# Score tiles as four matmuls of 32 columns, and the maximum pass's causal mask in 64-row matmuls

## What is computed

```python
def ffn(h):                       # weights are +1/-1 from booleans, widths 256 -> 1024 -> 1024 -> 256
    h = relu(s0 * (concat(h, -h) @ sign(k0))) * 2
    h = relu(s1 * (h @ sign(k1))) * 2
    return s2 * (h @ sign(k2))
def attn(h):                      # q, k, v: 16 heads of 16
    scores = where(causal, -1e9, q @ k.T / sqrt(16))
    return (softmax(scores) @ v) @ w_o.T + b_o
x = x + 0.5 * ffn(layernorm(x))
x = x + attn(layernorm(x))
x = x + 0.5 * ffn(layernorm(x))
```

## Time and profile before

| | |
|---|---|
| timed runs | 1733.23, 1733.54, 1737.15 us |
| profiled execution, first to last instruction | span 1730.6 us |
| TensorE matmul busy | 1669.8 us, 96% |
| VectorE busy | 1161.4 us, 67% |
| ScalarE busy | 959.1 us, 55% |
| GpSimd busy | 159.8 us, 9% |
| mean granted TensorE clock | 0.987 |
| attention stretch | 475 to 1348.8 us of the span |

### The profile page before, as it was taken

One profiled execution on the slowest core, in us unless ns is written; L12 is line 12 of the kernel. 1 busy time (PEld: TensorE's weight loads), 2 busy tenths in 40 slices (PEclk: granted clock), 3 DMA queues, 4 the chain that ended last, 5 costly groups with the idle time before them and its releaser, 6 DMA issues.

```text
span 1730.6 us, 31369 instructions
## 1 busy us (share of the span) xinstructions
PE 1669.8 (96%) x9872; PEld 691.9 (40%) x9872; DVE 1161.4 (67%) x1746; ACT 959.1 (55%) x1703; POOL 159.8 (9%) x310
## 2 busy tenths in 40 slices
PE   6899999999999999999999999999999799999999
PEld 3455555554522222222222222222223355555554
DVE  7535554455588887887887878878887566666632
ACT  2223322232288887888887878878888322222221
POOL 5100000000011110111111111011111000000000
PEclk9999999999999999999999999999999899999999
DMA  5011013110222201221122202221123111112000
GB/s 167 0 49 49 24 24 85 48 48 0 84 70 56 56 29 49 62 56 35 42 56 57 62 19 52 62 57 46 33 53 110 69 49 49 48 48 101 20 6 19
DMA packets 115754, 88.83 MB, mean 51 GB/s; under 512 B 76080, under 2 KB 95152, under 8 KB 115632
## 3 DMA queue, kind: packets, MB, share of 16 engines
q1 hardware_dynamic: 115632, 87.20, 17.3%
HBM read 49.15 MB, written 37.75 MB: 50 GB/s over the span
## 4 chain that ended last, share of the span: by engine, by line
PE 93%; DVE 3%; DMA 1%; issue 1%; SPq 1%; ACT 0%; DVEq 0%
PE ffn_mm L399 25%; PE ffn_mm L1184 17%; PE ffn_mm L1203 16%; PE ffn_mm L387 7%; PE ffn_acc L415 6%; PE ffn_acc L567 5%; PE ffn_tr L567 5%; PE ffn_mm L664 3%; PE ffn_tr L571 2%; PE ffn_acc L676 2%; PE ffn_acc L487 1%; PE ffn_tr L374 1%; PE ffn_acc L571 1%; DVE qk L1263 1%; DVE m_part L586 1%
## 5 line engine op out<-in xcount | busy, mean ns | idle before, releaser
L1145 ACT ACTIVATE probs<-ffn_mm,exp_scale 128x512 f32<-128x512 f32 (+3 forms) x1280 | 715.3, 636 | 134.8 <-PE ffn_mm L1184 129.0
L586 DVE TENSOR_REDUCE m_part<-ffn_acc 128x2 f32<-128x1024 f32 (+1 forms) x314 | 351.1, 1118 | 96.9 <-PE ffn_acc L567 53.4
L1184 PE MATMUL ffn_mm<-qk 66*128 66x512 f16 (+7 forms) x1280 | 389.5, 358 | 17.8 <-issue 14.1
L399 PE MATMUL ffn_mm<-ffn_h1h,w 128*128 128x512 f16 x1024 | 389.4, 380 | 7.7 <-DVE ffn_h2l L452 7.7
L399 PE MATMUL ffn_mm<-ffn_h1l,w 128*128 128x512 f16 x1024 | 389.3, 380 | 0.0
L586 DVE TENSOR_REDUCE m_part<-ffn_tr 128x2 f32<-128x1024 f32 (+3 forms) x326 | 328.0, 1006 | 40.7 <-PE ffn_tr L571 27.0
L1203 PE MATMUL ffn_mm<-probs,v 128*32 128x512 f32 (+3 forms) x2560 | 315.6, 550 | 0.3
L445 ACT ACTIVATE ffn_h2h<-ffn_mm 128x512 f16<-128x512 f32 x128 | 76.1, 597 | 309.5 <-PE ffn_mm L399 294.7
L1184 PEld LDWEIGHTS ffn_mm<-qk 66*128 66x128 f16 (+1 forms) x1280 | 103.8, 97 | 303.7 <-ACT probs L1145 232.1
L452 DVE SCALAR_TENSOR_TENSOR ffn_h2l<-ffn_mm,ffn_h2h 128x512 f16<-128x512 f32 x128 | 86.2, 686 | 191.6 <-ACT ffn_h2h L445 191.6
L1098 POOL TENSOR_SCALAR_AFFINE_SELECT probs<-probs 128x256 f32<-128x256 f32 (+1 forms) x256 | 109.8, 429 | 782.5 <-ACT probs L1145 782.4
(11 more groups left out here) (95 smaller groups left out, 1080.4 us busy)
## 6 DMA issues: line engine op xcount, KB each, us to landing
qk<-qk_scr SPq DMA_DIRECT2D x256, 64.0 KB, 2.7
ctx_scr<-ctx_out SPq DMA_DIRECT2D x64, 256.0 KB, 2.4
qk<-ctx_scr SPq DMA_DIRECT2D x64, 256.0 KB
v_scr<-v_pad SPq DMA_DIRECT2D x32, 256.0 KB, 2.9
v<-v_scr SPq DMA_DIRECT2D x16, 512.0 KB, 4.5
x_res<-L_attn_x SPq DMA_DIRECT2D x8, 512.0 KB, 3.6
qk_scr<-qk_hi SPq DMA_DIRECT2D x32, 128.0 KB, 1.8
qk_scr<-qk_lo SPq DMA_DIRECT2D x32, 128.0 KB, 1.8
```

What stands on the lines that cost most here:

```text
L399: ins = nc.tensor.matmul(f.mm[:, m % 4, :], w1[:, kt, m * P:(m + 1) * P], part[:, kt, :], start=(kt == 0 and part is f.h1h), stop=(kt == H ...
L586: nc.vector.tensor_reduce(m_part[u][:, t, :, r], s_ps[slot][:, :, 0:w], AX.X, ALU.max).then_inc(sb.s_done, 1)
L1145: nc.scalar.activation(probs[:, g % P_SLOTS, j, c0:CH], st_ps[bank(k)][:, c0:CH], ACT.Exp, scale=exp_scale[:, 0:1]).then_inc(se.exp_done, 1)
L1184: nc.tensor.matmul(st_ps[bank(k)][:, c0:CH], k_part(u, h, rows, slice(kb * P, (kb + 1) * P)), q_part(u, h, rows, slice(i * CH + c0, (i + 1 ...
```

## The change

Three edits. The score matmul of the second pass becomes four matmuls, each with 32 of the 128 keys as output columns, at column positions 0, 32, 64, 96, with the same moving operand and into the same bank; the semaphore is counted up on the last. The mask matmuls of the maximum pass become 64-row matmuls in each head's own rows, two halves for each head, with operands `pick_row` and `mask_row` in place of `ident_mask` and `mask`: four matmuls where there were two. GpSimd builds those operands after its other constants, and TensorE waits for them before the last feed-forward chunk; `mask` lives only in the first stage.

```diff
--- before.py
+++ after.py
@@ -120,6 +120,7 @@
 
         self.zero = new("zero")
         self.consts = new("consts")
+        self.pick = new("pick")
         self.vones = new("vones")
 
         self.sgn = new("sgn")
@@ -273,8 +274,8 @@
         bo_row = sbuf(top, "bo_row", [P, D], F32)
         ident = sbuf(top, "ident", [P, P], F32)
         ident_h = sbuf(top, "ident_h", [P, P], F16)
-        ident_mask = sbuf(top, "ident_mask", [P, P], F16)
-        mask = sbuf(top, "mask", [P, P], F16)
+        pick_row = sbuf(top, "pick_row", [P, 2, P], F16)
+        mask_row = sbuf(top, "mask_row", [P, 2, P], F16)
         ffn_scale = sbuf(top, "ffn_scale", [P, 1], F32)
         qk_scale = sbuf(top, "qk_scale", [P, 2], F32)
         exp_scale = sbuf(top, "exp_scale", [P, 1], F32)
@@ -567,9 +568,10 @@
                     ins = nc.tensor.matmul(s_ps[slot][:, h, 0:w], q_part(u, h, HEAD_ROWS[h], slice(t * P, (t + 1) * P)),
                                            k_part(u, h, HEAD_ROWS[h], slice(r * CH, r * CH + w)), start=True, stop=(r < i))
                 if r == i:
-                    for h in range(2):
-                        ins = nc.tensor.matmul(s_ps[slot][:, h, w - P:w], ident_mask[:, :], mask[:, :],
-                                               start=False, stop=True)
+                    for hf in range(2):
+                        for h in range(2):
+                            ins = nc.tensor.matmul(s_ps[slot][:, h, w - P:w], pick_row[HEAD_ROWS[h], hf, :],
+                                                   mask_row[HEAD_ROWS[h], hf, :], start=False, stop=(hf == 1))
             else:
                 wait(nc.tensor, sb.m_cols, cols)
                 ins = nc.tensor.matmul(s_ps[slot][0:4 * TPC, 0, 0:P], m_col.rearrange("p h a t -> p (h a t)"), ident_h[:, :],
@@ -621,6 +623,7 @@
             w_in = sbuf(st, "w_in", [P, 4, DT, D], F32)
             w_diff = sbuf(st, "w_diff", [P, DT, HID], F16)
             s_in = sbuf(st, "s_in", [P, 3], F32)
+            mask = sbuf(st, "mask", [P, P], F16)
             sgn = sbuf(st, "sgn", [P, 3], F32)
             s_abs = sbuf(st, "s_abs", [P, 3], F32)
             s_prod = sbuf(st, "s_prod", [P, 2], F32)
@@ -763,7 +766,6 @@
                                         pattern=[[-1, P]], channel_multiplier=1).then_inc(se.consts, 1)
                 pool.wait_ge(se.consts, 2)
                 nc.gpsimd.tensor_copy(ident_h[:, :], ident[:, :]).then_inc(se.consts, 1)
-                nc.gpsimd.tensor_scalar(ident_mask[:, :], ident[:, :], MASK_A, 0.0, ALU.mult, ALU.add).then_inc(se.consts, 1)
 
                 pool.wait_ge(se.k1_in, 16)
                 pool.wait_ge(se.sprep, 3)
@@ -782,6 +784,19 @@
                 pool.wait_ge(sb.rows_zero, 4)
                 for u in range(2):
                     nc.gpsimd.memset(k_part(u, 1, SHIFT_ROWS[1], slice(0, SEQ)), M_SCALE).then_inc(sb.rows_const, 1)
+
+                lo, hi = HEAD_ROWS
+                nc.gpsimd.memset(pick_row[:, :, :], 0.0).then_inc(se.pick, 1)
+                nc.gpsimd.memset(mask_row[:, :, :], 0.0).then_inc(se.pick, 1)
+                pool.wait_ge(se.pick, 2)
+                nc.gpsimd.memset(mask_row[hi, 0, 64:P], MASK_B).then_inc(se.pick, 1)
+                pool.wait_ge(se.pick, 3)
+                for n, (rows, hf, dst, src) in enumerate(((lo, 0, slice(0, P), slice(0, P)), (hi, 1, slice(0, P), slice(0, P)),
+                                                          (lo, 1, slice(64, P), slice(0, 64)), (hi, 0, slice(0, 64), slice(64, P)))):
+                    nc.gpsimd.tensor_scalar(pick_row[rows, hf, dst], ident[rows, src], MASK_A, 0.0, ALU.mult, ALU.add).then_inc(se.pick, 1)
+                    pool.wait_ge(se.pick, 2 * n + 4)
+                    nc.gpsimd.tensor_copy(mask_row[rows, hf, dst], mask[rows, src]).then_inc(se.pick, 1)
+                    pool.wait_ge(se.pick, 2 * n + 5)
 
                 pool.wait_ge(se.bo_in, 16)
                 with pool.Fori(0, NCH) as c:
@@ -1015,6 +1030,7 @@
                 with pe.Fori(1, NCH - 1) as c:
                     chunk(c)
                 pe.wait_ge(qk_in[0], 256)
+                pe.wait_ge(se.pick, 11)
 
 
                 c = NCH - 1
@@ -1181,8 +1197,11 @@
                             wait(pe, se.rows_in, (it * BODY_PAIRS + u) * (QCH * 32) + (i + 1) * 32)
                         wait(pe, se.exp_done, it * EXPS + bank_free(k))
                         rows = ALL_ROWS[h]
-                        nc.tensor.matmul(st_ps[bank(k)][:, c0:CH], k_part(u, h, rows, slice(kb * P, (kb + 1) * P)),
-                                         q_part(u, h, rows, slice(i * CH + c0, (i + 1) * CH)), start=True, stop=True).then_inc(se.st_ready, 1)
+                        for c in range(0, P, 32):
+                            ins = nc.tensor.matmul(st_ps[bank(k)][c:c + 32, c0:CH], k_part(u, h, rows, slice(kb * P + c, kb * P + c + 32)),
+                                                   q_part(u, h, rows, slice(i * CH + c0, (i + 1) * CH)), start=True, stop=True,
+                                                   tile_position=(0, c))
+                        ins.then_inc(se.st_ready, 1)
 
                     def products(g, body=0):
```

## The result

| | before | after |
|---|---|---|
| median of the timed runs | 1733.57 us (four runs) | 1687.51 us (1687.27 to 1689.23) |
| profiled span | 1730.6 us | 1685.7 us |
| TensorE busy | 1669.8 us | 1610.8 us |
| mean granted clock | 0.987 | 0.984 |

The ratio is 0.9728, 95% interval 0.9713 to 0.9743: 46 us faster, where 54 was forecast.

The account below looks back on a forecast made before the run. TensorE was taken to bound the kernel. Per pair, 4.4 us of saved switches less 0.4 for entries and 0.5 for waits gave 3.5; times 15.5 pairs, 54 us: about 1680 us, range 1660 to 1726.

Parts of the forecast that it names:

- The bound: Attention stage: TensorE sets the pace, busy 854.3 of 873.8 us, one head pair taking 54.6 us.
- A switch costs 0.10 us, and only where the shape changes: TensorE in attention: each array-shape change loses about 0.10 us; 114 a pair become 70, saving 4.4 us a pair.
- The lower value: Second-pass score matmul in four pieces: no extra streaming time, only 0.4 us a pair for entering column shape.
- The upper bound, by issue: Second-pass score matmul as eight instructions at 0.035 us each: 0.28 us, 0.06 over the 0.22 of one matmul.
- the argument for the semaphore: Score tile's semaphore on the last piece suffices, since the probability-times-value matmuls end in order and count the same way.
- What is late next: Attention pair at 50.6 us: short waits for ScalarE and VectorE take 0.5 us a pair, leaving net 3.5.
- Where the gain stops: Last pair, after the last turn at 1320.39: TensorE's savings there are lost, about half a pair, leaving 15.5 pairs.
- Weights exposed: Entries into column-shaped work: four weight loads cannot run ahead, costing 3.5 us a pair; 1726 us, chance 0.10.
- ScalarE or VectorE takes over: Attention pairs: another engine limits, the gain falls from 4.0 to 2 us a pair; 1702 us, chance 0.10.
- Pieces that do not run as one: Between first and fourth piece of each score matmul: 0.06 us extra by issue, slower at 1765 us, chance 0.10.
- the estimate of 1717: Score matmul's four pieces at about 62 ns each, by the Trainium skill: 0.25 us, 0.03 over 0.22; 1717 us.
- No effect: TensorE's 0.10 us loss belongs to a change of operands or bank, not shape: nothing gained, 1733 us, chance 0.05.

Follow-up runs that it names:

- the two halves: The kernel before with only the score matmuls in four 32-column pieces, 1702.18 us; the changed kernel with the score matmul whole again, mask edit kept, 1728.09 us.
- e_score_8: The changed kernel with every score piece cut again into two halves of the queries, eight matmuls a tile: 1699.50 us, ratio 0.9806.
- e_score_64: The changed kernel with the scores in two pieces of 64 columns instead of four of 32: 1740.72 us, ratio 1.0032.

## Why the prediction was right, point by point

**The bound.** TensorE's chain, read from distances between starts and not from busy time: right. Its busy share was 96% before and is 96% after, and says nothing of the 46 us.

**A switch costs 0.10 us, and only where the shape changes.** Right, and shown from three sides: score pieces of 32 columns lose it beside V, pieces of 64 keep it (0.33), and the mask loses it in 64 rows beside U and keeps it in the whole array (0.32 to 0.22). The count (114 to 70, 88 and 110 for the parts) gave 1702 to 1706 and 1727 for the two halves; 1702.2 and 1728.1 came out, in a set whose kernel before was 2.3 us slower than in the first. Over the whole stretch a switch is worth a little more than 0.10: from one unit to the next with S, V and S between, two switches fewer, the changed kernel saves 0.225 us (median of 88).

**What S costs in four pieces.** The lower value was right. S to V is 0.23, V without an entry of its own 0.86 instead of 0.88. The upper bound, by issue, was not near: twice the instructions again cost 0.009 a tile. The 0.02 that each entry into column-shaped work was to cost is smaller: from unit to unit with one 512-wide score tile between, 0.644 us became 0.652. And the argument for the semaphore, that the matmuls of V end in order, does not hold: in the kernel before, the V that starts at 821.57 counts up with an instruction that starts at 821.94, and two others start at 822.03. The same makes the last piece of S come early in 112 tiles.

**What is late next.** The term of 0.5 us a pair was named as waits for ScalarE and VectorE. 3.66 a pair came out (3.3 to 3.7 over three profiles), 0.34 under the 4.0. Halving the reductions brought none of it back, so the argument by their 1.13 us fell. The waits for VectorE that do exist stand behind the turns and take 0.19 a pair more than before. For ScalarE no new wait shows (3.4 us in both kernels), and it was not tried alone. That the term came out near its size is in part luck.

**Where the gain stops.** At the last turn the chain leaves TensorE, as before. The changed kernel's chain there:

```profile
1271.81 0.19 PE ffn_acc L577
...
1274.57 6.48 DVE qk L1282
...
1286.86 12.27 DMA qk<-ctx_scr
```

Up to T the start moved from 1320.39 to 1271.81, 48.6 us. After that, 3.7 us were given back: 3.3 by the load, 12.27 instead of 8.97, the rest at the start of the next stage.

**The term that was mis-sized** is one that the prediction did not have: the stops at the loop's branch, taken as unchanged. They went from 14.1 to 19.9. Summed by what was measured: 15.5 x 3.66 = 56.7, less 5.8 for the stops, less the 3.7 above, is 47.2, where the profiled spans differ by 44.9. Of the 2.3 left, some belongs to a stretch of 3.4 us from 480.8 us of the changed kernel in which the granted clock was 0.50, the lower level; there was none in that place before. The rest is within what 3.66 is good to. In the later profile of the same kernel the load is as short as before, and the sum closes: 15.5 x 3.31 = 51.3, less 4.7 for the stops, is 46.6, where the spans differ by 47.3. GpSimd's added constants and the masks in the early units cost nothing that shows.

**Rivals.** Weights exposed: S to U would have been above 0.40 and is 0.32, so no. The rule of the Trainium skill (TensorEngine Tiling (Array Packing), Restrictions), that column tiling disables Fast Weight Load, may hold, and no run here shows whether it does; whatever the four loads cost, it is behind the columns. ScalarE or VectorE takes over: 2 a pair was forecast for it and 3.66 is left. Pieces that do not run as one: refuted by 0.23; and eight matmuls in 0.23 us in `e_score_8`, 0.03 each, refute the estimate of 1717 that went by 0.25 for four. No effect: refuted by 46 us, and that it is the shape and no other property of a change of operands is shown by `e_score_64`, where S and V follow each other just as often and nothing is gained.

## What to carry over

List the array shapes of the matmuls (rows and columns of the weights) in the order in which they are issued and count the places where the shape changes; each cost 0.10 us here, a fifth of the attention stretch before. A matmul can be cut into the shape of its neighbours at next to no cost, but only into exactly that shape, and a change of one kind moves the switches of the next, so the parts must be counted together. And if a loop body is long, look at what its branch costs on each engine: writing out TensorE's and ScalarE's loops gave another 30 us (1687.5 to 1657.7), and with all loops written out the changed kernel took 1656.94 us, no different from that, 4.5% under the kernel before. Last, do not take it that pieces at different column positions end in program order: let each count its semaphore up.

## What the runs showed of the hardware that was not expected

A branch stopped TensorE for 2.6 to 3.0 us each time in the kernel before and for 3.0 to 4.4 in four profiles of the changed one. Where TensorE's loop was written out, ScalarE's own stops of up to 2.5 us came to light, and both had been hidden under one another. In the written-out code, eight bodies long instead of three, no such stop was seen.

A switch out of 64-column pieces costs 0.12 us, out of the whole array 0.10.

Matmuls at different column positions of one shape do not keep the order of the program where their widths differ: score pieces started up to 0.21 us before earlier pieces of the same tile.
